# One round of a block's second product ahead of the last four units of the next block's first product; smaller norm groups at the end; ScalarE makes and stores four of six outputs

## The chip, the cores and the metric

The kernel runs on one core of a Trainium2 chip. The metric is device time in microseconds (us), the median of several executions; one further execution was profiled, and all rows below come from that one. Engines are called by the names of the profile: PE (TensorE, matrix products; PEld its weight loads), DVE (VectorE), ACT (ScalarE), POOL (GpSimd) and SP (SyncE, which here only issues DMAs).

## The reference, cut to what matters

`x` is 5120 x 64, `adj` is 5120 x 5120 (105 MB in f32, nearly all zeros).

```
u = par_u[0] * par_u[1] * (diag_u[:, None] * x[:2048] @ W_u) + x[:2048]
i = par_i[0] * par_i[1] * (diag_i[:, None] * x[2048:] @ W_i) + x[2048:]
e = concatenate([u, i])
h = adj @ (adj.T @ e)
h = layernorm(h) * gamma + beta + x
y = layernorm(x + h)
out = layernorm(y + L1(y, adj))
```

`L1` is a graph layer whose edges survive only if softmax scores pass a threshold. The kernel finds the greatest row sum of squares of adj; below a limit no edge can survive, `L1` is zero, and the output is a further layernorm of `y`. With these inputs that is the case, so the program's branch for the message work is never entered.

## The kernel before, in words

Both products need the whole of adj, and adj is read from memory once. It is cut into ten **blocks** of 512 columns (c = 0 to 9). A block is 20 **units** of 512 KB, each two row tiles (256 rows) by 512 columns. On chip there are 40 slots for units, so two blocks fit: even blocks use slots 20 to 39, odd blocks slots 0 to 19, and a unit of block c+2 can be loaded only when its slot's unit of block c is done with.

What happens to a unit, in order:

1. SP issues its load (L977) after the wait `round_done`, that is, after the round that last read the slot.
2. ACT squares it and sums each row (`scan`, L1086), for the limit.
3. PE multiplies it into the **first product** adj.T @ e (`multiply_unit`, L1363), which accumulates over the 20 units of the block in one PSUM bank, `block_bank`.
4. DVE transposes it in place in 32 x 32 pieces (`turn_unit`, L1182), after PE and ACT have read it.

When all 20 units of block c+1 are multiplied, DVE turns the block's sum (`turn_half`, L1191), and ACT and POOL spread it into `col_sum` (`keep_cols`, L1095 and L1022). Then the **second product** of a block, adj @ (adj.T @ e), goes in **rounds** over the transposed units (`multiply_round`, L1382): rounds of 10, 14 and 16 row tiles (5, 7 and 8 units) for blocks 0 to 7, four rounds of 10 for block 8, five rounds of 8 for block 9. Here r0, r1, r2 are the rounds of a block; each leaves its result in four PSUM banks, lower (0 to 3) or upper (4 to 7), and DVE adds it to `h_sum` (`add_round`, L1204). A round waits until the last round in the same banks is added.

Every engine works in the order in which the code is written for it; there is no scheduler. On PE the order is: 20 units of block c+1, then all rounds of block c, then 20 units of block c+2, and so on. Blocks 0 and 1 are interleaved more finely (5 units, r0, 7 units, r1, 8 units, r2 of block 0). After r1 of block 0 PE makes a small product with gamma (L1427), for which ACT waits after its scan of unit 10 of block 1 (L1109).

The end: the rounds of block 9 alternate with `close_tiles` (L1395), which turns eight tiles of `h_sum` into natural rows, minus the mean. Norm group k (8 tiles) then goes: ACT squares (L1113), DVE sums and scales (L1264, L1266), POOL takes the power -1/2 (L1047, `root_c`), DVE multiplies and adds x (L1272, L1276), ACT squares (L1118), DVE sums and scales (L1282, L1285), POOL takes the power (L1052, `root_y`), DVE multiplies (`make_out`, L1293), SP stores (L988). x itself is loaded again once r0 of block 8 has freed its slots (L984), summed by DVE (L1251) and centred by POOL (`center_x`). After the last store has landed SP loads the flag that tells whether the message branch is entered (L407).

Of the kernel before, what the change touches and what calls it, by code (L numbers as in the profile page):

```python
# [7 lines left out]
def adjacency_layers_kernel(nc, x, adj, w_ui, scales, gamma, beta,  # L8
# [13 lines left out]
    P = 128  # L22
# [33 lines left out]
    LGROUPS = T // GT  # L56

# [25 lines left out]
    with ctx:  # L83
# [16 lines left out]
        def setup(width, parts=P):  # L100
# [13 lines left out]
        x_sum, c_sum, var, rstd, y_sum, y_var, y_eps, x1_rstd, scale = (  # L114
            pooled[:, x_at + T * D + T * i:x_at + T * D + T * i + T] for i in range(9))
        ln_at = x_at + T * D + 9 * T

        def ln_buffer(i):
            a = ln_at + GT * D * i
            return pooled[:, a:a + GT * D].rearrange("p (t d) -> p t d", d=D)  # L120

        assert ln_at <= x_at + CH * PARTS[NB - 2][0][1] and ln_at + 8 * GT * D <= x_at + CH * sum(PARTS[NB - 2][1])
        c_sq = [ln_buffer(0), ln_buffer(1)]
        y_sq = [ln_buffer(2), ln_buffer(3)]
        ln_t = [ln_buffer(4), ln_buffer(5)]
        ln_o = [ln_buffer(6), ln_buffer(7)]

# [75 lines left out]
        block_bank = bank[4:6]  # L203
# [36 lines left out]
        c_summed = sem("c_summed")  # L240
# [5 lines left out]
        y_summed = sem("y_summed")  # L246
        y_var_made = sem("y_var_made")
        scale_made = sem("scale_made")
        x1_steps = sem("x1_steps")
        out_made = sem("out_made")  # L250
        out_stored = [sem(f"out_stored{k}") for k in range(2)]
# [111 lines left out]
        def before_in_banks(g):  # L363

            return [r for r in range(g) if upper_banks(r) == upper_banks(g)]

        def nat_of(k):

            return pair[(0, 1, 0, 1, 2)[k]][:, :].rearrange("p (t d) -> p t d", d=2 * D)
# [31 lines left out]
        def over_row(ap):  # L401
            return ap.unsqueeze(2).to_broadcast([P, GT, D])
# [484 lines left out]
        def message_dve(dve):  # L887

            dve.wait_ge(out_stored[0], 16 * ((LGROUPS + 1) // 2))
            dve.wait_ge(out_stored[1], 16 * (LGROUPS // 2))  # L890
# [52 lines left out]
        def message_pool(pool):  # L943

            pool.sem_inc(ln_stored, 16)
            pool.wait_ge(y_summed, LGROUPS)
            for k in range(LGROUPS):
                nc.gpsimd.tensor_scalar(y_eps[:, group_tiles(k)], y_sum[:, group_tiles(k)], 1.0 / D, LN_EPS,
                                        ALU.mult, ALU.add).then_inc(x1_steps, 1)
# [11 lines left out]
        def _(sp):  # L961
# [24 lines left out]
            for k in range(LGROUPS):  # L986
                sp.wait_ge(out_made, k + 1)
                sp.dma_start(tile_rows(out, GT * k, GT), ln_o[k % 2][:, :, :]).then_inc(out_stored[k % 2], 16)  # L988
            sp.wait_ge(out_stored[0], 16 * ((LGROUPS + 1) // 2))
            sp.wait_ge(out_stored[1], 16 * (LGROUPS // 2))  # L990
            with sp.If(edges_may_survive(sp) > 0):
                message_sp(sp)

        @block.gpsimd
        def _(pool):
# [39 lines left out]
            def center_x(k):  # L1035
                xk = x_all[:, group_tiles(k), :]
                pool.wait_ge(x_steps, 1 + 3 * k)
                nc.gpsimd.tensor_tensor(xk, xk, over_row(x_sum[:, group_tiles(k)]), ALU.subtract).then_inc(x_steps, 1)
# [6 lines left out]
            def root_c(k):  # L1045
                pool.wait_ge(var_made, k + 1)
                nc.gpsimd.tensor_tensor(rstd[:, group_tiles(k)], var[:, group_tiles(k)], minus_half[:, :],  # L1047
                                        ALU.pow).then_inc(rstd_made, 1)

            def root_y(k):  # L1050
                pool.wait_ge(y_var_made, k + 1)
                nc.gpsimd.tensor_tensor(scale[:, group_tiles(k)], y_var[:, group_tiles(k)], minus_half[:, :],  # L1052
                                        ALU.pow).then_inc(scale_made, 1)

            for k in range(LGROUPS - 1):
                center_x(k)
            root_c(0)
            pool.wait_ge(rstd_made, 1)
            center_x(LGROUPS - 1)
            pool.wait_ge(x_steps, 1 + 3 * LGROUPS)  # L1060
# [4 lines left out]
            root_c(3)  # L1065
            root_c(4)
            root_y(2)
            root_y(3)
            root_y(4)
            with pool.If(edges_may_survive(pool) > 0):  # L1070
# [3 lines left out]
        def _(act):  # L1074
# [27 lines left out]
            for v in range(1, UNITS):  # L1102
# [4 lines left out]
                if c == 1 and i == UPB[c] // 2:  # L1107
                    act.wait_ge(gamma_turned, 1)
                    act.copy(center[:, D:2 * D], bank[7][:, 0:D]).then_inc(center_kept, 1)  # L1109

            def square_c(k):
                act.wait_ge(nat_made, k + 1)
                nc.scalar.activation(c_sq[k % 2][:, :, :], nat_of(k)[:, :, 0:D],  # L1113
                                     ACT.Square).then_inc(c_squared, 1)

            def square_y(k):
                act.wait_ge(y_made, k + 1)
                nc.scalar.activation(y_sq[k % 2][:, :, :], x_all[:, group_tiles(k), :],  # L1118
                                     ACT.Square).then_inc(y_squared, 1)
# [4 lines left out]
            act.wait_ge(c_summed, 1)  # L1124
# [361 lines left out]
```

## Time and profile before

| | us |
|---|---|
| median of 3 runs | 415.44 (413.74 to 416.66) |
| the profiled execution, device time | 414.27 |
| its span, first to last instruction | 412.5 |
| PE busy | 383.8 (93%) |
| DVE busy | 324.7 (79%) |
| ACT busy | 266.6 (65%) |
| POOL busy | 68.6 (17%) |
| DMA, share of 16 engines by adj and x loads | 72.6% |

The granted PE clock is at full speed (1.00) in each 20 us stretch up to 400 us. No engine is busy all of the time, so the totals alone do not tell what bounds the kernel; the rows below do.

### The profile page before, as it was taken

What the parts mean: (1) busy time and instruction counts of PE and PEld (TensorE: products, weight loads), DVE (VectorE), ACT (ScalarE), POOL (GpSimd) and SP (SyncE); (2) the same over time, 40 slices, a digit from 0 to 9 for tenths busy, and PEclk for the clock granted to TensorE, in tenths of its full rate; (3) what the DMA queues carried; (4) which work ended last, traced back from release to release, by engine and by line L of the source; (5) the groups of instructions that cost most, each with busy time, mean ns of one, the idle gap of its engine ahead of it and who ended that gap; (6) DMA issues with size and microseconds to landing.
All of it is one profiled execution on the core that took longest, in us unless ns stands there. A gap on an engine that the chain in (4) does not pass through costs nothing.

```text
span 412.5 us, 13885 instructions
## 1 busy us (share of the span) xinstructions
PE 383.8 (93%) x6018; PEld 223.2 (54%) x6018; DVE 324.7 (79%) x404; ACT 266.6 (65%) x497; POOL 68.6 (17%) x122
## 2 busy tenths in 40 slices
PE   8987999999999999999999999999999999999940
PEld 7543555565464455546445554644555464668740
DVE  3699769799695979769786966988696697694783
ACT  3696938799888488578848857884785688100220
POOL 2001100303003000300200030011003001169663
PEclk9999999999999999999999999999999999999995
DMA  8999999954992998399389929957992995400002
GB/s 293 386 387 381 386 386 387 382 217 144 388 386 109 322 387 314 114 388 385 138 289 379 354 83 373 387 184 260 385 370 55 392 386 202 130 4 3 29 27 82
DMA packets 56706, 109.87 MB, mean 266 GB/s; under 512 B 3776, under 2 KB 3904, under 8 KB 56640
## 3 DMA queue, kind: packets, MB, share of 16 engines
q1 hardware_dynamic: 56352, 108.84, 72.6%
q8 instruction: 49, 0.80, 0.8%
q10 hardware_dynamic: 288, 0.09, 0.1%
q14 instruction: 17, 0.14, 0.1%
HBM read 107.60 MB, written 1.31 MB: 264 GB/s over the span
## 4 chain that ended last, share of the span: by engine, by line
PE 51%; DMA 23%; SPq 18%; DVE 2%; issue 2%; POOL 1%; ACT 0%; DVEq 0%; ACTq 0%
PE pair L1382 39%; DMA pooled<-in_adj 22%; SPq L977 17%; PE pair L1363 10%; PE pair L1395 2%; DMA pooled<-in_x 2%; POOL pooled L1052 1%; DVE pooled L1204 1%; SPq L968 1%; DVE pooled L1182 1%; SPq L963 1%; POOL pooled L1047 0%; DVE pooled L1272 0%; DVE pooled L1264 0%; DVE pooled L1293 0%
## 5 line engine op out<-in xcount | busy, mean ns | idle before, releaser
L1086 ACT ACTIVATE scratch<-pooled 128x1024 bf16<-128x1024 f32 x200 | 210.5, 1053 | 63.8 <-DMA pooled<-in_adj 61.9
L1182 DVE STREAM_TRANSPOSE pooled<-pooled 128x1024 f32<-128x1024 f32 x200 | 228.8, 1208 | 11.3 <-ACT scratch L1086 8.9
L1363 PE MATMUL pair<-pooled,rows_in 128*64 128x256 f32 x1600 | 186.0, 383 | 10.7 <-DMA pooled<-in_adj 10.3
L1382 PE MATMUL pair<-pooled,col_sum 32*64 32x320 f32 (+3 forms) x4224 | 177.4, 485 | 0.9 <-DVE pooled L1204 0.5
L1363 PEld LDWEIGHTS pair<-pooled,rows_in 128*64 128x64 f32 x1600 | 109.6, 137 | 88.4 <-DMA pooled<-in_adj 31.1
L1382 PEld LDWEIGHTS pair<-pooled,col_sum 32*64 32x64 f32 x4224 | 94.0, 132 | 78.7 <-issue 57.0
L1204 DVE TENSOR_TENSOR pooled<-pooled,pair 128x320 f32<-128x320 f32 (+3 forms) x120 | 58.1, 545 | 44.6 <-PE pair L1382 44.6
L1022 POOL COPY col_sum<-col_half 32x256 f32<-32x256 f32 x80 | 31.6, 394 | 317.6 <-DVE col_half L1191 314.6
L1095 ACT COPY col_sum<-col_half 32x256 f32<-32x256 f32 x80 | 32.2, 403 | 11.1 <-DVE col_half L1191 10.3
L1086 ACT ACTIVATION_READ_ACCUMULATOR scratch<-pooled 128x1 f32 x200 | 37.4, 187 | 0.0
L1113 ACT ACTIVATE pooled<-pair 128x512 f32<-128x512 f32 x5 | 3.0, 598 | 39.3 <-PE pair L1395 39.3
L1191 DVE STREAM_TRANSPOSE col_half<-pair 128x256 f32<-128x256 f32 x10 | 4.4, 438 | 14.4 <-PE pair L1363 14.4
L1395 PEld LDWEIGHTS pair<-center,pooled 128*128 128x128 f32 x80 | 9.2, 192 | 1.5 <-issue 1.5
L1395 PE MATMUL pair<-center,pooled 128*128 128x128 f32 x80 | 10.0, 280 | 0.0
L1047 POOL TENSOR_TENSOR pooled<-pooled,minus_half 128x8 f32<-128x8 f32 x5 | 8.6, 1723 | 6.1 <-DVE pooled L1266 5.9
L1052 POOL TENSOR_TENSOR pooled<-pooled,minus_half 128x8 f32<-128x8 f32 x5 | 8.5, 1710 | 0.7 <-DVE pooled L1285 0.7
L1080 ACT COPY pooled<-pair 128x512 f32<-128x512 f32 x5 | 2.8, 587 | 8.7 <-PE pair L1335 8.7
L1042 POOL TENSOR_TENSOR pooled<-pooled,beta_sb 128x512 f32<-128x512 f32 x5 | 6.7, 1342 | 0.4
L1202 DVE COPY pooled<-pair 128x320 f32<-128x320 f32 (+2 forms) x12 | 6.3, 585 | 0.1
L1118 ACT ACTIVATE pooled<-pooled 128x512 f32<-128x512 f32 x5 | 3.1, 629 | 4.4 <-DVE pooled L1276 4.4
L1156 DVE TENSOR_TENSOR rows_in<-pair,pooled 128x256 f32<-128x256 f32 x10 | 3.7, 410 | 2.9 <-PE pair L1345 2.6
L1345 PE MATMUL pair<-pooled 64*128 64x64 f32 x80 | 5.5, 278 | 0.3 <-ACT pooled L1080 0.3
(47 smaller groups left out, 62.2 us busy)
## 6 DMA issues: line engine op xcount, KB each, us to landing
pooled<-in_adj SPq DMA_DIRECT2D x200, 512.0 KB, 10.1
pooled<-in_x SPq DMA_DIRECT2D x5, 256.0 KB, 3.7
out<-pooled SPq DMA_DIRECT2D x5, 256.0 KB, 2.0
pooled<-in_x SPq DMA_DIRECT2D x1, 768.0 KB, 6.9
pooled<-in_x SPq DMA_DIRECT2D x1, 512.0 KB, 3.7
pooled<-in_w_ui ACTq DMA_DIRECT2D x1, 64.0 KB, 2.9
beta_sb<-in_beta SPq DMA_DIRECT2D x1, 32.0 KB, 9.0
pooled<-in_scales ACTq DMA_DIRECT2D x1, 22.0 KB, 3.2
```

The lines of the kernel that those rows point to most:

```text
L977: sp.dma_start(slots[slot_of(v)].rearrange("p (t k) -> p t k", t=ut), tile_rows(adj, ut * i, ut)[:, :, c0:c0 + WIDTHS[c]]).then_inc(unit_l ...
L1022: kept = nc.gpsimd.tensor_copy(spread_to(c, a, 1, f), spread_from(c, 1, f))
L1042: nc.gpsimd.tensor_tensor(xk, xk, beta_sb[:, :].unsqueeze(1).to_broadcast([P, GT, D]), ALU.add).then_inc(x_steps, 1)
L1047: nc.gpsimd.tensor_tensor(rstd[:, group_tiles(k)], var[:, group_tiles(k)], minus_half[:, :], ALU.pow).then_inc(rstd_made, 1)
L1052: nc.gpsimd.tensor_tensor(scale[:, group_tiles(k)], y_var[:, group_tiles(k)], minus_half[:, :], ALU.pow).then_inc(scale_made, 1)
L1086: nc.scalar.activation(scratch[v % 2][:, :], slots[slot_of(v)], ACT.Square, accum_out=square_sum[:, v:v + 1]).then_inc(unit_scanned, 1)
L1095: kept = act.copy(spread_to(c, a, 0, f), spread_from(c, 0, f))
L1182: nc.vector.transpose(tiles, tiles).then_inc(unit_turned, 1)
L1204: added = nc.vector.tensor_tensor(to, to, share, ALU.add)
L1363: mm = pe.matmul(block_bank[c % 2][half(h), 0:w // 2], rows_in[:, t, :], slots[slot_of(v)][:, at:at + w // 2], start=(t == 0), stop=(t == ...
L1382: mm = pe.matmul(round_banks(g)[a][half(b % 2), 0:w].rearrange("p (t r) -> p t r", r=32), col_sum[c % 2][quadrant(a), b, :], to[quadrant(a ...
L1395: mm = pe.matmul(nat_of(k)[:, i, :], h_sum[:, P * t:P * t + P], center[:, :], start=True, stop=True)
```

## The change

Five things are changed.

1. **Order on PE.** For every block from 1 to 8, r0 of block c stands behind the first 16 units of block c+1 instead of behind all 20; the last four units follow, then r1 and r2. Block 8 now has the rounds 10, 14, 16 too. Block 0's r2 stands behind the first two units of block 2 (`AHEAD`). DVE's order follows.
2. **Banks.** The first product's bank and the banks of the rounds are chosen so that r0 and r1 of a block use the half in which the block's own first product was, r2 the other. So r1 now waits for `add_round` of r0, and r2 for `turn_half` of the block that was just multiplied.
3. **Groups at the end.** Block 9 has rounds and norm groups of 8, 8, 8, 8, 4 and 4 tiles instead of five of 8.
4. **Norm steps.** The factor 1/D is taken into ACT's square, and a 65th column holds epsilon, so that one `tensor_reduce` replaces the reduce and the small `tensor_scalar` (L1266 and L1285 are gone). POOL writes those columns with four small memsets.
5. **Outputs.** The first four output groups are made by ACT, one `activation` of 128 x 64 per tile, and stored from ACT's queue; DVE makes and SP stores only the last two, of 4 tiles. SP loads the flag before it waits for the stores. ACT's wait for gamma moves from behind unit 10 to behind unit 16 of block 1.

The diff, cut to its core:

```diff
-    PARTS = [((0, 10), (10, 14), (24, 16))] * (NB - 2)
-    PARTS += [tuple((t, 10) for t in range(0, T, 10)), tuple((t, 8) for t in range(0, T, 8))]
+    PARTS = [((0, 10), (10, 14), (24, 16))] * (NB - 1)
+    PARTS += [((0, 8), (8, 8), (16, 8), (24, 8), (32, 4), (36, 4))]
+    AHEAD = 2
+        def banks_of_block(c):
+            return c % 2 == 0
         def upper_banks(g):
             c = place_of_round(g)[0]
             if c == NB - 1:
-                return g > LAST
-            return c > 0 and (g - ROUNDS_AT[c]) % 2 == 1
+                return banks_of_block(NB - 2) == (g == LAST)
+            return banks_of_block(c) == (g < ROUNDS_AT[c + 1] - 1)
...
-                if c == 1 and i == UPB[c] // 2:
+                if c == 1 and i == 16:
                     act.wait_ge(gamma_turned, 1)
...
+            def make_out(k):
+                act.wait_ge(scale_made, k + 1)
+                for i in range(norm_size(k)):
+                    t = norm_tiles(k).start + i
+                    made = nc.scalar.activation(ln_o[k % 4][:, i, :], x_all[:, t, :], ACT.Copy, scale=scale[:, t:t + 1])
+                made.then_inc(out_made_act, 1)
+                act.wait_ge(out_made_act, k + 1)
+                store_out(act, k)
...
             def sum_c(k):
                 dve.wait_ge(c_squared, k + 1)
-                tiles = group_tiles(k)
-                nc.vector.tensor_reduce(c_sum[:, tiles], c_sq[k % 2][:, :, :], X, ALU.add).then_inc(c_summed, 1)
-                dve.wait_ge(c_summed, k + 1)
-                nc.vector.tensor_scalar(var[:, tiles], c_sum[:, tiles], 1.0 / D, LN_EPS,
-                                        ALU.mult, ALU.add).then_inc(var_made, 1)
+                nc.vector.tensor_reduce(var[:, norm_tiles(k)], c_sq[k % 2][:, 0:norm_size(k), :], X,
+                                        ALU.add).then_inc(var_made, 1)
...
             for c in range(1, NB - 1):
-                for v in range(UNIT_FIRST[c + 1], UNIT_FIRST[c + 2]):
+                first = UNIT_FIRST[c + 1]
+                for v in range(first + AHEAD if c == 1 else first, first + 16):
                     multiply_unit(v)
-                for g in rounds_of(c):
-                    multiply_round(g)
+                multiply_round(ROUNDS_AT[c])
+                for v in range(first + 16, first + 20):
+                    multiply_unit(v)
+                multiply_round(ROUNDS_AT[c] + 1)
+                multiply_round(ROUNDS_AT[c] + 2)
```

In the middle of the program, PE's order for one block before: L1363 are the units of block c+1 (four matmuls each), L1382 the rounds of block c, 64x320 being r0, 64x448 r1 and 64x512 r2.

```order
L1363 MATMUL pair<-pooled,rows_in 64x256 x80
L1382 MATMUL pair<-pooled,col_sum 64x320 x64
L1382 MATMUL pair<-pooled,col_sum 64x448 x64
L1382 MATMUL pair<-pooled,col_sum 64x512 x64
L1363 MATMUL pair<-pooled,rows_in 64x256 x80
```

The same place now (the lines are L1411 and L1431):

```order
L1411 MATMUL pair<-pooled,rows_in 64x256 x64
L1431 MATMUL pair<-pooled,col_sum 64x320 x64
L1411 MATMUL pair<-pooled,rows_in 64x256 x16
L1431 MATMUL pair<-pooled,col_sum 64x448 x64
L1431 MATMUL pair<-pooled,col_sum 64x512 x64
L1411 MATMUL pair<-pooled,rows_in 64x256 x64
```

r0 moved ahead of 16 matmuls, the last four units. DVE's order for one block before, in the same place (L1182 transposes, L1191 `turn_half`, L1204 `add_round`):

```order
L1182 STREAM_TRANSPOSE pooled<-pooled 128x1024 x13
L1191 STREAM_TRANSPOSE col_half<-pair 128x256
L1182 STREAM_TRANSPOSE pooled<-pooled 128x1024 x2
L1204 TENSOR_TENSOR pooled<-pooled,pair 128x10x32 x4
L1182 STREAM_TRANSPOSE pooled<-pooled 128x1024 x5
L1204 TENSOR_TENSOR pooled<-pooled,pair 128x14x32 x4
L1204 TENSOR_TENSOR pooled<-pooled,pair 128x16x32 x4
```

and now (L1233, L1242, L1255):

```order
L1233 STREAM_TRANSPOSE pooled<-pooled 128x1024 x13
L1255 TENSOR_TENSOR pooled<-pooled,pair 128x10x32 x4
L1233 STREAM_TRANSPOSE pooled<-pooled 128x1024
L1242 STREAM_TRANSPOSE col_half<-pair 128x256
L1233 STREAM_TRANSPOSE pooled<-pooled 128x1024 x5
L1255 TENSOR_TENSOR pooled<-pooled,pair 128x14x32 x4
L1233 STREAM_TRANSPOSE pooled<-pooled 128x1024
L1255 TENSOR_TENSOR pooled<-pooled,pair 128x16x32 x4
```

The add of r0 moved ahead of `turn_half`. The end of PE's program before, from the last round (64x256) on; L1395 is `close_tiles`, L1447 the turn of the greatest sums:

```order
L1382 MATMUL pair<-pooled,col_sum 64x256 x64
L1395 MATMUL pair<-center,pooled 128x128 x16
L1447 MATMUL pair<-ident,part_max 1x128
```

and now, from the first round of 4 tiles (64x128) on; the last 16 closing matmuls are split around a round:

```order
L1431 MATMUL pair<-pooled,col_sum 64x128 x64
L1444 MATMUL pair<-center,pooled 128x128 x8
L1431 MATMUL pair<-pooled,col_sum 64x128 x64
L1444 MATMUL pair<-center,pooled 128x128 x8
L1506 MATMUL pair<-ident,part_max 1x128
```

## Rows read from the trace of the kernel before

**Rows 1.** The page, chain that ended last: shares of the span by line

```profile
PE pair L1382 39%; DMA pooled<-in_adj 22%; SPq L977 17%; PE pair L1363 10%; PE pair L1395 2%; DMA pooled<-in_x 2%; POOL pooled L1052 1%; DVE pooled L1204 1%; SPq L968 1%; DVE pooled L1182 1%; SPq L963 1%; POOL pooled L1047 0%; DVE pooled L1272 0%; DVE pooled L1264 0%; DVE pooled L1293 0%
```

**Rows 2.** The chain in order of time, 200 to 245 us: start, length, what

```profile
202.68 17.46 PE pair L1382 x384
...
226.65 11.43 DMA pooled<-in_adj
...
238.12 1.08 PE pair L1363 x8
```

**Rows 3.** The chain in order of time, 40 to 112 us

```profile
43.56 4.49 PE pair L1382 x128
48.05 6.20 PE pair L1363 x56
54.25 6.20 PE pair L1382 x128
60.81 7.06 PE pair L1363 x64
67.87 7.05 PE pair L1382 x128
74.92 17.42 PE pair L1363 x160
92.34 17.46 PE pair L1382 x384
```

**Rows 4.** The chain over the whole span: the rounds of blocks 2 and 7

```profile
129.66 17.46 PE pair L1382 x384
...
312.14 17.46 PE pair L1382 x384
```

**Rows 5.** ACT in order of time: scans of units 0 and 17, one block

```profile
211.65 1.06 ACT L1086 ACTIVATE scratch<-pooled 128x1024 bf16<-128x1024 f32 x1 [5.13 <-DMA pooled<-in_adj]
...
235.53 1.06 ACT L1086 ACTIVATE scratch<-pooled 128x1024 bf16<-128x1024 f32 x1 [0.20 <-DMA pooled<-in_adj]
```

**Rows 6.** DVE in order of time, the same block

```profile
207.28 1.68 DVE L1204 TENSOR_TENSOR pooled<-pooled,pair 128x320 f32<-128x320 f32 x4 [1.85 <-PE pair L1382]
...
222.56 14.75 DVE L1182 STREAM_TRANSPOSE pooled<-pooled 128x1024 f32<-128x1024 f32 x13
```

**Rows 7.** ACT, then DVE, in order of time around ACT's wait for gamma

```profile
60.84 0.21 ACT L1109 COPY center<-pair 128x64 f32<-128x64 f32 x1 [6.89 <-PE pair L1427]
...
62.21 1.25 DVE L1182 STREAM_TRANSPOSE pooled<-pooled 128x1024 f32<-128x1024 f32 x1 [3.69 <-ACT scratch L1086]
63.38 2.18 DVE L1202 COPY pooled<-pair 128x448 f32<-128x448 f32 x4
65.48 9.11 DVE L1182 STREAM_TRANSPOSE pooled<-pooled 128x1024 f32<-128x1024 f32 x8
```

**Rows 8.** PE in order of time, end: a round of 8 tiles, last closes; PEld of that round

```profile
370.20 3.95 PE L1382 MATMUL pair<-pooled,col_sum 32*64 32x256 f32 x128 [0.52 <-DVE pooled L1204]
...
392.73 3.84 PE L1395 MATMUL pair<-center,pooled 128*128 128x128 f32 x32
...
370.17 3.53 PEld L1382 LDWEIGHTS pair<-pooled,col_sum 32*64 32x64 f32 x128 [0.94 <-issue]
```

**Rows 9.** Groups by line and shape: busy us, mean ns

```profile
L1047 POOL TENSOR_TENSOR pooled<-pooled,minus_half 128x8 f32<-128x8 f32 x5 | 8.6, 1723 | 6.1 <-DVE pooled L1266 5.9
...
L1032 POOL TENSOR_SCALAR pooled<-pooled 128x40 f32<-128x40 f32 x1 | 0.3, 316 | 10.8 <-DVE pooled L1251 10.8
```

**Rows 10.** The end: last output on DVE, landing of the five stores, SP's flag load

```profile
406.26 0.69 DVE L1293 TENSOR_TENSOR pooled<-pooled 128x512 f32<-128x512 f32 x1 [0.55 <-POOL pooled L1052]
...
DMA to landing us min/median/max: 2.0/2.0/3.9
...
L407 SPq TENSOR_LOAD <-flag x1: 472/472/472, 410.9 to 410.9; - x1
L407 SPq FUSED_REGOPS  x1: 191/191/191, 411.4 to 411.4; - x1
```

More of the change, by code:

```diff
@@ L113, in adjacency_layers_kernel, with ln_buffer @@
         x_all = pooled[:, x_at:x_at + T * D].rearrange("p (t d) -> p t d", d=D)
[L114 to L126, printed above, removed]
+        x_sum, var, rstd, y_var, y_eps, x1_rstd, scale = (
+            pooled[:, x_at + T * D + T * i:x_at + T * D + T * i + T] for i in range(7))
+        ln_at = x_at + T * D + 7 * T
+        ln_end = [ln_at]
+        def ln_buffer(width):
+            ln_end[0] += GT * width
+            return pooled[:, ln_end[0] - GT * width:ln_end[0]].rearrange("p (t d) -> p t d", d=width)
+        c_sq = [ln_buffer(D + 1) for _ in range(2)]
+        y_sq = [ln_buffer(D + 1) for _ in range(2)]
+        ln_t = [ln_buffer(D) for _ in range(2)]
+        ln_o = [ln_buffer(D) for _ in range(4)]
+        assert ln_at <= x_at + CH * PARTS[NB - 2][0][1] and ln_end[0] <= x_at + CH * sum(PARTS[NB - 2][1])
         rows_in = sb("rows_in", [P, T, D])
@@ L984, in _ @@
                 sp.dma_start(x_all[:, a:b, :], tile_rows(x, a, b - a)).then_inc(x_again, 16)
[L986 to L991, printed above, removed]
+            for k in range(BY_ACT, NORMS):
+                sp.wait_ge(out_made, k - BY_ACT + 1)
+                store_out(sp, k)
+            survives = edges_may_survive(sp)
+            for k in range(4):
+                sp.wait_ge(out_stored[k], 16 * len(range(k, NORMS, 4)))
+            with sp.If(survives > 0):
                 message_sp(sp)
@@ L1220, in _ @@
                 turn_unit(v)
[L1223 to L1230 removed]
+            for v in range(UNIT_FIRST[1], UNIT_FIRST[1] + 5):
+                turn_unit(v)
+            add_round(0)
+            make_gamma_and_beta()
+            for v in range(UNIT_FIRST[1] + 5, UNIT_FIRST[1] + 12):
+                turn_unit(v)
@@ L1233, in _ @@
+            add_round(1)
+            for v in range(UNIT_FIRST[1] + 12, UNIT_FIRST[1] + 18):
+                turn_unit(v)
+            turn_half(1)
+            for v in range(UNIT_FIRST[1] + 18, UNIT_FIRST[2] + AHEAD):
+                turn_unit(v)
+            add_round(2)
             for c in range(1, NB - 1):
                 first = UNIT_FIRST[c + 1]
-                for v in range(first, first + 13):
-                    turn_unit(v)
-                turn_half(c + 1)
-                for v in range(first + 13, first + 15):
+                for v in range(first + AHEAD if c == 1 else first, first + 13):
@@ L1239, in _ @@
                     turn_unit(v)
                 add_round(ROUNDS_AT[c])
-                if c < NB - 2:
-                    for v in range(first + 15, UNIT_FIRST[c + 2]):
+                turn_unit(first + 13)
+                turn_half(c + 1)
+                if c == NB - 2:
+                    for v in range(first + 14, first + 16):
+                        turn_unit(v)
+                    dve.wait_ge(x_again, 16 * 2)
+                    nc.vector.tensor_reduce(x_sum[:, :], x_all[:, :, :], X, ALU.add).then_inc(x_summed, 1)
+                    add_round(ROUNDS_AT[c] + 1)
+                    for v in range(first + 16, UNITS):
+                        turn_unit(v)
+                else:
+                    for v in range(first + 14, first + 19):
```

212 lines of the change are left out of this document (111 added, 101 removed).

## The prediction

> **What bounds the kernel now.** I first read the chain that ended last. PE holds about half of it, all in products and rounds, and nearly 40% is loads of adj and SP's queue at L977 [rows 1]. So neither PE nor the DMA engines bound it alone; they take turns. The chain in order of time shows how. The rounds of one block are followed by a load, and then by only one unit (eight matmuls) before the next rounds start [rows 2]: the last unit of the product waits for its load, and that load was released by r0 of the block before. The cycle in numbers: r0 starts at 202.68 and lasts 4.49 [rows 3], so it ends at 207.17; the last of the 20 units that it releases lands at 238.08; its unit takes 1.08 and the next r0 starts at 239.20. That is 4.49 + 30.9 + 1.1 = 36.5 us for a block. The rounds of blocks 2 and 7 stand five blocks apart, 129.66 and 312.14 [rows 4]: 182.48/5 = 36.5 again. The same work without waits is 17.42 for 20 units and 17.46 for three rounds [rows 3], 34.9. So a block loses 1.6 us, because the DMA queue stands empty from the last landing to the first landing after r0 (211.65, 4.5 us after r0's end [rows 5]).
>
> **The middle.** r0 now comes four units earlier, 4 x 0.87 = 3.5 us, and frees five slots. The other 15 are freed by r1 and r2, which stand where they stood. What matters more is that the units before the next r0 are 16, not 20. I go round the new cycle from the end of r1. The first landing comes 4.5 us later, as above. The scans of units 0 and 17, which follow the landings, stand 23.88 us apart [rows 5], 1.40 a unit. Units 0 to 4 were released by r0, so units 5 to 15 are needed: unit 15 lands at 4.5 + 10 x 1.40 = 18.5. Then it is multiplied (1.1), r0 follows (4.5), four units (3.5) and r1 (6.2): 33.8 us from r1 to r1. The last four land by 24.1 and are used by 28. The PE's own work is 34.9, so PE becomes the bound with 1.1 us to spare, and the wait is gone.
>
> PE pays something for it: one more change per block between products and rounds. Block 0 shows its price. r0, 7 units, r1, 8 units, r2 take 4.49 + 6.20 + 6.20 + 7.06 + 7.05 = 31.0; 15 units in a row at 0.871 and three rounds in a row are 13.07 + 17.46 = 30.53 [rows 3]. So two more changes cost 0.47, one 0.24, and a block will take 34.88 + 0.24 = 35.1. The Trainium skill has a rule here that speaks against the change: "TensorEngine Tiling (Array Packing)", Key Properties, says that a change of tiling mode drains TensorE, and products and rounds use different modes. The trace agrees in sign, and 0.24 us is what it shows; by that page the eight more changes are a loss of some 2 us, which is in the sum already.
>
> DVE must not take PE's place. In a block it has 20 transposes, of which 13 take 14.75, so 22.7; the adds of r0 and r1 take 1.7 and 2.2, r2's by the same step 2.5, and `turn_half`, a quarter of a transpose's width, some 0.4: 29.5 of 35.1 [rows 6, 7]. The add of r0 is now waited for by r1. DVE starts the 13 transposes 2.5 us into the product, ends them at 17.3, and r0 ends at 18.4: it is there in time, adds until 20.1, and r1 starts at 21.9. r2 waits for `turn_half`, done at some 22.4, and starts at 28. Both waits cost nothing; the cover is 1.8 and 5 us. ACT spreads the columns later than before, while the five early units land. Its scans keep up with landings of 1.40 [rows 5], so 20 take at most 28 of 35.1 and leave 7 for the copies; only transposes queue behind them.
>
> From 109.80 (end of block 1's rounds) to 329.60 (end of block 7's) are six blocks. The first took 147.12 - 109.80 = 37.32, the others 182.48. Six at 35.12 are 210.7 where 219.8 were: **-9.1 us**.
>
> **The start.** r2 of block 0 now needs `turn_half` of block 1. PE reaches it at 60.81 + 10 x 0.88 = 69.6. DVE: ACT stood 6.89 us for gamma and DVE 3.69 for ACT; with the wait behind unit 16 that is gone. So the add of r1 runs from 60.5 to 62.7, six transposes (9.11/8 each) to 69.5, the half to 69.9 [rows 7]. PE waits 0.4 (if ACT still held DVE, up to 3). With the extra change of block 1: **+0.7 us**.
>
> **The end.** Before, from 329.60 to 412.5, 82.9 us; PE is done at 396.57, 67.0 into it [rows 8]. Now: 35.1 to the end of block 8's r2; two rounds of 8 tiles 7.9; three closes and two more such rounds, 2.0 + 3.95 + 2.0 + 3.95 + 2.0 = 13.9, to 56.9; then a round of 4, a close of 8, a round of 4 and two closes of 4. What a round of 4 costs is not in the trace. Half the columns would be 2.0; the same number of instructions at their pace is 3.95. Weight loads are the same 128 in both; in a round of 8 they run for 3.53 us [rows 8]. I take 3.7, nearest to that row. Then 56.9 + 3.7 + 2.0 + 3.7 + 2.1 = 68.4: PE ends 1.4 us later than before. The load of x lies beside r1 and the four units, and no longer stops PE (the 0.52 before the round of 8 goes).
>
> Weighed against a page: the Trainium skill, "TensorE: Matmul & The Clock Gate", LDWEIGHTS, says that a weight load depends on its columns alone, and its Back-to-back issue gap that small matmuls never start closer than 25 ns. By that 128 of them take 3.2 us, 0.5 less than I take each time, and the sum would be 1 us lower.
>
> Behind PE only half as many tiles wait. DVE's operation of 512 columns takes 0.69 [rows 10]; for 256, on ACT too, I take 0.4. So a square and a sum, 0.8, then POOL without a pause: powers for c4, c5, y3, y4, y5. A power of 8 columns takes 1.7. For 4 columns the bounds are 0.85 (half) and 1.7 (no less); a plain POOL operation of 40 columns takes 0.3, so the rest hangs on the columns, and I take 1.0 [rows 9]. So 4 x 1.0 + 1.7 = 5.7, the last output on DVE 0.4, hops 0.5: 75.8. Landing took 2.0 to 3.9 [rows 10]; I take 2.4 for 128 KB. The last store was issued at 407.0 and landed at 410.9; of the 1.6 from there to 412.5 SP's flag load and register work (0.47 + 0.19) now lie beside the landing, leaving 0.9. Sum 79.1, **-3.8 us**. ACT's outputs: its copy of 128 x 64 took 0.21 [rows 7], so 1.7 a group of 8, beside DVE and POOL: nothing. The last such group starts when POOL has made y3, two powers of 4 before the end, so it may take 2.4 before its store comes after SP's. The dropped `tensor_scalar`s, memsets and ACT's store issues lie beside other work and are in the figures above.
>
> **Sum.** -9.1 + 0.7 - 3.8 = -12.2 on the profiled execution's 414.27: 402.1. The median of the runs stands 1.2 above that execution; I add half, **402.7 us**. A measurement here tells about 1% from no change.
>
> **Rivals.**
> - *Rounds of 4 cost by width*: 2.0 instead of 3.7, twice: 399.3. For it speaks that matmuls of 320 columns and more cost by width; against it that 8 tiles (3.95) cost more than 8/10 of r0's 4.49. Chance 0.15.
> - *Powers do not shrink*: four of POOL's five at 1.7, +2.8, 405.5. POOL is the last link either way. Chance 0.14.
> - *A new wait takes back 1 us a block*: PE waits for `add_round` of r0 or for unit 15, since the spare time is only 1.8 and 1.1 us. Seven blocks, 409.7. Chance 0.07.
> - *The change does not do what it says*: PE's queue is strictly in order, so if the moved r0 itself waits (for its columns or its add), units still end last and a block stays at 36.5. Left are start and end, -3.1, 411.8. Against it: its columns are spread over 25 us before. Chance 0.03.
> - *Slower than before*: the loads now come in two bursts, one after r0 and one after r1, and the queue restarts twice. If that made the pace of landing worse, unit 15 would be late: a block takes 19.8 + 10 x pace. At 1.53 it equals PE, at 1.67 the old 36.5, from there the kernel loses. At 1.85 a block takes 38.3, +1.8 in seven blocks, 12.6 - 3.1: 424.4. Against it: scans follow landings at 1.40 across r0, r1 and r2 alike. Chance 0.02.
> - The forecast: 0.59, its own range 400.5 to 405.
>
> **Range and chances.** 398.5 to 408.5 takes in the first two rivals and half of the third. Faster by over 1% (below 411.3) are the forecast and the first three, 0.95; within 1% the fourth, 0.03; slower 0.02.
>
> **What would show it.** In the profile after, PE's idle time behind adj loads in the middle is near zero and r0 starts of neighbouring blocks stand 35.1 apart (34.9 if changes are free, 36.5 if the loads still rule). r2 of block 0 shows a wait of half a microsecond. Rounds of 4 tiles stand with 128 matmuls in some 3.7 us, POOL's powers of 4 columns with 1.0. From PE's last matmul to the end are 11 us, where 15.9 were. The prediction fails if PE is seen waiting for `add_round` or `turn_half` in each block, or if ACT holds a square back behind its outputs.

## The result and the profile after

The changed kernel took **400.49 us** (median, 398.13 to 401.76) beside 415.85 us (413.74 to 416.66) for the kernel before on the same chip. The ratio is **0.963**, 95% interval 0.957 to 0.969. The profiled execution took 400.99 us with a span of 399.2, where 414.27 and 412.5 stood before: 13.3 us less. Of the runs below, two executions, 409.04 (r0 behind 18 units) and 416.96 (more to load, changed order), count as slow, and the ratios leave them out; without them the medians of these two runs are 406.43 and 414.31.

The page of the kernel after, the chain that ended last, shares by engine and by line; it answers to [rows 1]:

```profile
PE 86%; SPq 8%; DMA 3%; issue 1%; ACT 1%; POOL 0%; DVE 0%; ACTq 0%; POOLq 0%
PE pair L1431 44%; PE pair L1411 39%; SPq L1008 6%; DMA pooled<-in_adj 3%; PE pair L1444 3%; SPq L999 1%; SPq L994 1%; ACT pooled L1167 0%; POOL pooled L1084 0%; ACT pooled L1160 0%; SPq L1000 0%; DVE pooled L1332 0%; DVE pooled L1340 0%; PE pair L1477 0%; ACTq L429 0%
```

The loads have fallen from 39% of the chain to 9%, and what is left of them lies ahead of 44 us. The first products (L1411) went from 10% to 39% of it: not more work, but work that used to lie hidden ahead of a late load.

The chain of the kernel after in order of time (start, length, what), which answers to [rows 2 to 4]:

```profile
44.65 4.49 PE pair L1431 x128
...
61.90 8.78 PE pair L1411 x80
70.68 0.39 issue
71.07 7.13 PE pair L1431 x128
78.20 12.24 PE pair L1411 x112
90.44 4.49 PE pair L1431 x128
94.93 3.60 PE pair L1411 x32
98.53 13.07 PE pair L1431 x256
111.60 13.96 PE pair L1411 x128
125.56 4.49 PE pair L1431 x128
...
322.36 13.96 PE pair L1411 x128
336.32 4.49 PE pair L1431 x128
340.81 3.60 PE pair L1411 x32
344.42 19.97 PE pair L1431 x512
```

Between 71 and 388 us the chain stays on PE, but for 1.8 us of "issue" in the last rounds. A block is 16 units, r0, four units, r1 and r2: 13.96 + 4.49 + 3.60 + 13.07 = 35.12 us, without a gap. From r0 of block 2 (125.56) to r0 of block 8 (336.32) are 210.76 us, six times 35.13; the same rounds stood 36.5 apart before [rows 4]. The only wait in the middle is the 0.39 us at 70.68, r2 of block 0 behind `turn_half`.

PE in order of time, kernel after, the end (start, us, what, idle before it); it answers to [rows 8]:

```profile
366.30 3.71 PE L1431 MATMUL pair<-pooled,col_sum 32*64 32x256 f32 x128
...
371.94 4.09 PE L1431 MATMUL pair<-pooled,col_sum 32*64 32x256 f32 x128
...
377.95 1.63 PE L1431 MATMUL pair<-pooled,col_sum 32*64 32x128 f32 x95
381.25 0.70 PE L1431 MATMUL pair<-pooled,col_sum 32*64 32x128 f32 x33 [1.67 <-issue]
381.88 2.05 PE L1444 MATMUL pair<-center,pooled 128*128 128x128 f32 x16
383.87 2.43 PE L1431 MATMUL pair<-pooled,col_sum 32*64 32x128 f32 x128
386.22 2.20 PE L1444 MATMUL pair<-center,pooled 128*128 128x128 f32 x16
```

The first round of 4 tiles needed 1.63 + 0.70 of work, with a stall of 1.67 us in its middle whose releaser is "issue": nothing that the profile shows held PE. Then ACT and POOL behind PE, in order of time, which answer to [rows 9, 10]:

```profile
389.26 2.01 ACT L1167 ACTIVATE pooled<-pooled 128x64 f32<-128x64 f32 x8
391.30 0.34 ACTq L429 DMA_DIRECT2D out<-pooled  x1
391.74 0.72 ACT L1160 ACTIVATE pooled<-pooled 128x256 f32<-128x256 f32 x2 [0.47 <-ACT pooled L1167]
```

```profile
388.95 1.98 POOL L1079 TENSOR_TENSOR pooled<-pooled,minus_half 128x4 f32<-128x4 f32 x2 [0.34 <-DVE pooled L1317]
390.90 3.77 POOL L1084 TENSOR_TENSOR pooled<-pooled,minus_half 128x8 f32<-128x8 f32 x3
```

POOL's last five powers follow each other from 388.95 to 394.67. The second row joins one of 8 columns and two of 4. The chain runs through ACT's outputs (L1167), because the square at 391.74 stood behind them, but POOL was busy until 392.5 and took the result at 392.69, so this costs at most 0.2 us.

### The profile page after: what moved, and what is told of

Same layout as the page of the kernel before. It is cut to its first block, busy times and chain, and to the rows that moved or that the text cites. A ratio compares the mean times of both kernels' runs of the same rounds, so it can differ in the third digit from the quotient of the medians.

```text
span 399.2 us, 13910 instructions
## 1 busy us (share of the span) xinstructions
PE 380.1 (95%) x6018; PEld 222.6 (56%) x6018; DVE 321.5 (81%) x395; ACT 271.9 (68%) x531; POOL 68.5 (17%) x128
## 4 chain that ended last, share of the span: by engine, by line
PE 86%; SPq 8%; DMA 3%; issue 1%; ACT 1%; POOL 0%; DVE 0%; ACTq 0%; POOLq 0%
PE pair L1431 44%; PE pair L1411 39%; SPq L1008 6%; DMA pooled<-in_adj 3%; PE pair L1444 3%; SPq L999 1%; SPq L994 1%; ACT pooled L1167 0%; POOL pooled L1084 0%; ACT pooled L1160 0%; SPq L1000 0%; DVE pooled L1332 0%; DVE pooled L1340 0%; PE pair L1477 0%; ACTq L429 0%
## 5 line engine op out<-in xcount | busy, mean ns | idle before, releaser
L1122 ACT ACTIVATE scratch<-pooled 128x1024 bf16<-128x1024 f32 x200 | 210.1, 1051 | 38.1 <-DMA pooled<-in_adj 36.7
L1233 DVE STREAM_TRANSPOSE pooled<-pooled 128x1024 f32<-128x1024 f32 x200 | 229.6, 1207 | 7.9 <-ACT scratch L1122 7.9
L1411 PE MATMUL pair<-pooled,rows_in 128*64 128x256 f32 x1600 | 181.3, 381 | 4.9 <-DMA pooled<-in_adj 4.8
L1431 PE MATMUL pair<-pooled,col_sum 32*64 32x320 f32 (+4 forms) x4224 | 178.9, 486 | 2.2 <-issue 1.7
L1411 PEld LDWEIGHTS pair<-pooled,rows_in 128*64 128x64 f32 x1600 | 111.7, 137 | 76.1 <-issue 11.7
L1431 PEld LDWEIGHTS pair<-pooled,col_sum 32*64 32x64 f32 x4224 | 90.9, 132 | 83.3 <-issue 66.4
L1255 DVE TENSOR_TENSOR pooled<-pooled,pair 128x320 f32<-128x320 f32 (+4 forms) x120 | 58.4, 548 | 46.7 <-PE pair L1431 46.5
L1152 ACT ACTIVATE pooled<-pair 128x512 f32<-128x512 f32 (+1 forms) x6 | 3.2, 526 | 31.3 <-PE pair L1444 31.3
L1079 POOL TENSOR_TENSOR pooled<-pooled,minus_half 128x8 f32<-128x8 f32 (+1 forms) x6 | 8.6, 1435 | 8.7 <-DVE pooled L1317 8.6
L1242 DVE STREAM_TRANSPOSE col_half<-pair 128x256 f32<-128x256 f32 x10 | 4.4, 441 | 5.7 <-PE pair L1411 5.7
L1084 POOL TENSOR_TENSOR pooled<-pooled,minus_half 128x8 f32<-128x8 f32 (+1 forms) x6 | 8.5, 1430 | 0.1
L1167 ACT ACTIVATE pooled<-pooled 128x64 f32<-128x64 f32 x32 | 8.0, 335 | 0.1
```

Source lines behind the costliest of these rows:

```text
L1079: nc.gpsimd.tensor_tensor(rstd[:, norm_tiles(k)], var[:, norm_tiles(k)], minus_half[:, 0:norm_size(k)], ALU.pow).then_inc(rstd_made, 1)
L1084: nc.gpsimd.tensor_tensor(scale[:, norm_tiles(k)], y_var[:, norm_tiles(k)], minus_half[:, 0:norm_size(k)], ALU.pow).then_inc(scale_made, 1)
L1122: nc.scalar.activation(scratch[v % 2][:, :], slots[slot_of(v)], ACT.Square, accum_out=square_sum[:, v:v + 1]).then_inc(unit_scanned, 1)
L1167: made = nc.scalar.activation(ln_o[k % 4][:, i, :], x_all[:, t, :], ACT.Copy, scale=scale[:, t:t + 1])
L1233: nc.vector.transpose(tiles, tiles).then_inc(unit_turned, 1)
L1255: added = nc.vector.tensor_tensor(to, to, share, ALU.add)
```

## The experiments

They ran in three series; each kernel is compared with the kernel before on its own chip (413.84, 414.52 and 414.27 us). The changed kernel ran again in the second and the third, not in the first, so the first series gives ratios only. Each trace is one execution.

**The changed kernel again.** 

> The changed kernel itself, for comparison on the chip of this series: its ratio to before should be 0.957 to 0.969 as in the first result, with blocks 35.1 us apart. If it comes out near 0.975 instead, the chip matters and the runs with the early gamma wait and with r0 behind 18 units lost less than they seemed to (they gave 0.976 and 0.980).

> The changed kernel again, on the chip of this series, as the base of the three runs beside it: 0.957 to 0.974 of before.

401.15 us (398.86 to 401.96), ratio 0.968 (0.962 to 0.974), and 401.16 us (399.59 to 402.70), ratio 0.970 (0.963 to 0.977). So the gain is 3 to 3.7%, and two kernels that differ by less than some 0.7% can't be told apart here. In the first repeat the first round of 4 tiles had a stall of 1.40 (time in which PE does nothing and waits for nothing that the profile shows, "issue"); in the second it had none:

```profile
378.46 2.10 PE L1431 MATMUL pair<-pooled,col_sum 32*64 32x128 f32 x128
380.49 2.05 PE L1444 MATMUL pair<-center,pooled 128*128 128x128 f32 x16
```

From start to start that round took 2.03 us.

**The end alone.** Order and banks of before, with the groups, the norm steps and ACT's outputs of the change. The core of the edit against the changed kernel:

```diff
-    PARTS = [((0, 10), (10, 14), (24, 16))] * (NB - 1)
-    PARTS += [((0, 8), (8, 8), (16, 8), (24, 8), (32, 4), (36, 4))]
+    PARTS = [((0, 10), (10, 14), (24, 16))] * (NB - 2)
+    PARTS += [tuple((t, 10) for t in range(0, T, 10)), ((0, 8), (8, 8), (16, 8), (24, 8), (32, 4), (36, 4))]
...
-                if c == 1 and i == 16:
+                if c == 1 and i == UPB[c] // 2:
```

> The end of the changed kernel (groups of 8, 8, 8, 8, 4, 4, fused norm steps, ScalarE's outputs, flag loaded early) behind the middle of the kernel before (old order, old banks, block 8 in four rounds, gamma wait at unit 10). My theory: the two parts are additive, and the end alone brings what the two traces show from the end of block 7's rounds on, 82.9 - 76.8 = 6 us, less what block 8 brought of it (its unit waits 1.8, a shorter tail of rounds 0.5), so 3 to 4.5 us: about 411.5 against 415.5 of before, with blocks still 36.5 us apart. Rival: the end gained only because the middle delivers x and the rounds earlier (before, PE waited 0.5 us behind the sum of x), then this run is within 1 us of before.

411.63 us (409.66 to 414.38, 10 runs), ratio 0.994 (0.991 to 0.998): 0.6%, some 2.4 us, less than the 3 to 4.5 that were expected. Its chain in order of time shows the middle of before, a load and eight matmuls ahead of each set of rounds, here 36.35 us apart and 36.6 in the mean of blocks 2 to 7:

```profile
130.28 17.46 PE pair L1430 x384
...
154.16 11.35 DMA pooled<-in_adj
...
166.63 17.46 PE pair L1430 x384
```

Its end, from 330.7 to 411.5, is 80.8 us long, 2.1 less than before. Both of its rounds of 4 tiles stalled, here in the order of time of PE:

```profile
388.93 1.57 PE L1430 MATMUL pair<-pooled,col_sum 32*64 32x128 f32 x89
392.19 0.91 PE L1430 MATMUL pair<-pooled,col_sum 32*64 32x128 f32 x39 [1.69 <-issue]
...
396.96 1.14 PE L1430 MATMUL pair<-pooled,col_sum 32*64 32x128 f32 x56 [0.59 <-issue]
```

**The order alone.** Order, banks, gamma wait and the fused norm steps of the change; five groups of 8, DVE's outputs and the late load of the flag of before. The core of the edit:

```diff
-    PARTS += [((0, 8), (8, 8), (16, 8), (24, 8), (32, 4), (36, 4))]
+    PARTS += [tuple((t, 8) for t in range(0, T, 8))]
...
-    BY_ACT = 4
+    BY_ACT = 0
```

> The middle of the changed kernel (order, banks, three rounds for block 8, gamma wait at unit 16) with the end of before: five groups of 8, VectorE makes and SP stores all outputs, flag loaded behind the stores; the fused norm steps stay. My theory: the middle brings 8.3 us to the end of block 7 (35.1 instead of 36.5 a block) and about 2 us in block 8, so 405 to 406, and together with the run of the end alone it makes the whole 15 us. Rival (the parts overlap: the end would hide part of what the middle gains, or the reverse): the two gains together miss the whole by more than 2 us.

404.94 us (403.25 to 405.20), ratio 0.975 (0.968 to 0.982). This part carries four fifths of the gain of the two runs. They add up within the noise: 0.6% and 2.5% are 3.1%, where the whole gave 3.0 to 3.7%. But the fused norm steps are in both runs, so what they bring is counted twice, and no run has them alone. Its blocks stand 35.13 us apart, except one of 36.17 with a late load. Block 7's rounds end at 322.74 and the span at 403.4, so its end is 80.7 us long, where 82.9 stood before and 76.8 after. So in these traces 2.2 of the end's 6.1 us come with the order and the fused norm steps (PE's 0.52 us behind the load of x [rows 8] is one part), and the small groups and ACT's outputs bring 3.9 on top of them. With the order of before all the steps of the end together brought 2.1 us (above), so their worth hangs on the order.

**The wait for gamma left at unit 10.**

```diff
-                if c == 1 and i == 16:
+                if c == 1 and i == 10:
```

> The changed kernel with one number back: ScalarE waits for gamma behind unit 10 of block 1, not 16. My theory: ScalarE stands about 7 us, VectorE's 7th transpose of that stretch waits until 63, the add of r1 and turn_half come 3 us later, and PE's wait for turn_half before r2 of block 0 grows from 0.4 to about 3 us; the whole kernel is about 2.7 us longer (403.3 against 400.5), since PE is the bound from there on and nothing gives it back. Rival: the later loads have room enough behind r2 of block 0, so the delay is taken up by block 1 and the time stays within 1 us.

> The early gamma wait again, now beside the changed kernel on the same chip. In its first trace PE waited 3.17 us for turn_half, 2.8 more than the changed kernel. If that is all, it is 2.8 us (0.7%) longer than the changed kernel here; the first series gave 4 to 6 us against a changed kernel of another chip. If it is 5 us again, something behind r2 of block 0 loses as well (the later loads of block 2, or late loads in block 3).

406.10 us (402.15 to 407.86), ratio 0.976 (0.968 to 0.985), and again 404.25 us (403.03 to 405.91), ratio 0.975 (0.969 to 0.982), 3.1 us more than the changed kernel beside it. The repeat's PE, in order of time:

```profile
73.49 8.82 PE L1431 MATMUL pair<-pooled,col_sum 32*64 32x512 f32 x128 [3.17 <-DVE pooled L1233]
```

r2 of block 0 waits 3.17 us where it waited 0.39, and then takes 8.82 us instead of 7.13. That is not more work: behind the wait PE's granted clock fell to half, 1.2 instead of 2.4 GHz, from 74.2 to 77.6 us. The windows view of that stretch (times; busy us and number of instructions of PE, PEld, DVE, ACT and POOL; granted clock; DMA share; GB/s):

```profile
74.20:77.60 3.40, 3.40 (x40) 1.54 (x32) 1.44 (x2) 3.30 (x8) 2.45 (x7) 0.50 0.85 311
```

3.4 us at half the clock cost 1.7, which is 8.82 - 7.13. The first run's trace shows the same: a wait of 3.17, half the clock from 73.2 to 76.6, and 8.43 us for r2. In the changed kernel, which waits 0.39 there, the clock stayed at 1.00. From r2 on the blocks follow each other at 35.13. So this execution, the slowest of its four, lost 2.8 us by the longer wait and 1.7 by the clock behind it, 4.5 in all; the medians stand 3.1 apart. The 0.4 us of the forecast rests on the moved line.

**r0 behind 18 units instead of 16.**

```diff
-                for v in range(first + AHEAD if c == 1 else first, first + 16):
+                for v in range(first + AHEAD if c == 1 else first, first + 18):
                     multiply_unit(v)
                 multiply_round(ROUNDS_AT[c])
-                for v in range(first + 16, first + 20):
+                for v in range(first + 18, first + 20):
```

DVE adds r0 behind 14 transposes instead of 13, directly ahead of `turn_half`.

> The changed kernel with r0 of a block behind 18 units of the next product instead of 16 (VectorE adds it behind 14 transposes instead of 13). My theory (a cycle of loads: from the end of r1 4.5 us to the first landing, 1.36 to 1.40 a unit, then unit, r0, the remaining units, r1): unit 17 lands 20.8 to 21.3 after r1, then 1.1 + 4.5 + 1.7 + 6.2 = 34.3 to 34.8, just below PE's 35.1, so the block stays at 35.1 to 35.4 us, with loads as PE's last wait now and then and a small wait of r1 for the add of r0 (0 to 0.2): 400.5 to 402.5. Rival: any unit behind r0 is enough to hide the loads, and the time is 400.5 as before with no wait at all; other rival: the bank handover costs a full add (1.7 us less 1.7 of the two units, plus hops) in each block, 0.3 x 8 = 2.4 us or more.

> r0 behind 18 units again, now beside the changed kernel. The cycle of loads has some 0.3 us to spare by the average pace, and the traces show single landings 1.2 us late; so by my theory it loses in the executions in which they fall badly, 1 to 6 us more than the changed kernel, with a wider spread (402 to 409 in the first series, the profiled one being its fastest). Rival (18 is as good as 16, and the first series saw its chip): within 1 us.

406.61 us (402.34 to 409.04, 6 runs), ratio 0.980 (0.973 to 0.987), and 406.97 us (405.43 to 407.35), ratio 0.982 (0.975 to 0.988), 5.8 us more than the changed kernel beside it; 400.5 to 402.5 was expected. Of the seven distances between its r0 in the repeat four are 35.3 to 36.0 us and three 36.5 to 37.5; the mean is 36.1. In the long ones PE waits again for single units ahead of r0:

```profile
162.00 1.08 PE L1410 MATMUL pair<-pooled,rows_in 128*64 128x256 f32 x8 [0.26 <-DMA pooled<-in_adj]
163.34 1.08 PE L1410 MATMUL pair<-pooled,rows_in 128*64 128x256 f32 x8 [0.26 <-DMA pooled<-in_adj]
164.35 4.56 PE L1430 MATMUL pair<-pooled,col_sum 32*64 32x320 f32 x128
```

So having some units behind r0 is not enough; their number counts. Each unit more ahead of r0 adds one landing to the cycle and takes 0.88 us of product out of its rest. With 16, unit 15 came 0.4 us before PE wanted it (below), so that cycle was 34.7 us. At the 1.56 us for a landing that were measured there, 18 units make it 34.7 + 2 x (1.56 - 0.88) = 36.1. That the mean is 36.1 too is partly chance. The seven distances hold 6.8 us more than seven of 35.13. The loads account for half of it, some 3.4. Rounds that took 13.91 and 14.80 us (with a stall of 0.69) instead of 13.14 account for 2.4, and a longer way from r0 to r1 and through r1 and r2, 0.13 in each block, for the rest. Why the rounds stretched is not shown; the granted clock was 1.00 there.

**r0 behind 12 units.** The same edit with 12, DVE adding r0 behind 10 transposes.

> The changed kernel with r0 behind 12 units of the next product instead of 16, eight behind it (VectorE adds it behind 10 transposes). My theory: PE is the bound at 35.1 us a block, so a profiled execution without late loads is as long as the changed kernel's, within 1 us. But the cycle of loads has 1.1 us to spare behind 16 units and about 3 us behind 12 (unit 11 lands at 4.5 + 6 x 1.4 = 12.9, then 1.1 + 4.5 + 7.0 + 6.2 = 31.7), and the traces show single loads that land 1.2 us or more late; so the waits for adj in the middle vanish in every execution, and the spread of the times shrinks. The rival theory is that all that matters is that units stand behind r0: then 12, 16 and 18 give the same.

399.95 us (399.50 to 400.66), ratio 0.966 (0.961 to 0.971), beside 401.15 for 16 units. The intervals overlap, so it is not shown to be faster. PE has no wait for adj behind 84 us in its trace, as was expected. Its times spread over 1.2 us, the 16's over 3.1 in the same series. Its r0 stand 35.12 or 35.13 us apart, the first two here:

```profile
86.22 4.49 PE pair L1432 x128
...
121.34 4.49 PE pair L1432 x128
```

The cycle by loads is 4 x (1.56 - 0.88) = 2.7 us shorter than with 16 units. That brings no time, since PE's work is the floor.

**More to load.** From block 2 on, each unit's load is followed in SP's queue by a copy of 64 KB that nothing needs, an eighth more bytes; once with the changed order, once with that of before.

```diff
+                if c >= 2:
+                    sp.dma_start(tile_rows(pruned, ut * i, 1)[:, 0, c0:c0 + P],
+                                 tile_rows(adj, ut * i, 1)[:, 0, c0:c0 + P]).then_inc(spare_loaded, 16)
```

> The changed kernel with 64 KB more DMA traffic behind each unit's load from block 2 on, a copy of a part of adj into a scratch tensor in memory that nothing reads (it also writes 64 KB, so the cost is between 12% and 25% of a unit's load: a landing every 1.53 to 1.70 us). My theory, from the cycle 19.8 + 10 x pace: 35.1 to 36.8 us a block, so 0 to 12 us longer in seven blocks. Rival (PE alone bounds it, the loads are hidden whatever they cost): no change.

> The kernel before with the same extra traffic. My theory: its cycle holds 20 landings in a row, 4.5 + 4.5 + 19 x pace + 1.1, so each block grows by 19 times the pace's growth: 39.2 to 42.4 us instead of 36.5, 19 to 41 us longer in all, at least twice what the changed kernel loses. Rival (both are bound by the DMA engines' total, and the change only removed a constant idle time): both grow alike.

Changed order: 414.70 us (410.28 to 416.96, 8 runs), ratio 0.999 (0.995 to 1.003), 13.5 us more than without the copies, a little beyond the expected 0 to 12. Order of before: 442.09 us, ratio 1.068 (1.061 to 1.075), 27.6 us more. Chains in order of time, the changed order first, then that of before:

```profile
126.73 4.49 PE pair L1435 x128
...
346.94 4.49 PE pair L1435 x128
```

```profile
214.30 17.46 PE pair L1386 x384
...
254.54 17.46 PE pair L1386 x384
...
294.81 17.46 PE pair L1386 x384
```

A block takes 36.7 us in the first (220.2/6) and 40.3 in the second: 1.6 and 3.8 more than without. The order of before pays for every slower landing; the changed one has a little cover first, and beyond it pays for the ten steps from unit 5 to unit 15, where the other pays for nineteen. The sizes fit: 3.8/19 is 0.20 us for a landing, and 10 x 0.20 less the 0.4 of cover (below) is 1.6.

**Block 9's rounds of 8 in two passes of 4.** Four rounds are made of 256 narrow matmuls instead of 128:

```diff
+                cuts = 2 if c == NB - 1 and nt == 8 else 1
+                for cut in range(cuts):
+                    t0, t1 = nt // cuts * cut, nt // cuts * (cut + 1)
```

> The changed kernel with each of block 9's four rounds of 8 tiles made in two passes of 4 tiles (128 matmuls and weight loads each, same results), which measures what a round of 4 costs. If the cost goes by width, as the one undisturbed round of 4 seen so far suggests (2.03 us, against 3.64 for 8 tiles), two passes take 4.1 us and the kernel grows by 4 x 0.4 = 1.8 us at most. If it goes by the number of instructions (3.6 a pass), it grows by 14 us. If the stall inside a round of 4 (1.4 to 1.7 us without any releaser in four of five traces) is PE running out of instructions that come too slowly, eight passes in a row must show more and longer such stalls, some 1.5 us in every second pass, 6 us in all.

409.85 us (two runs), 8.7 us more than the changed kernel beside it, ratio 0.990 (0.982 to 0.998). PE in order of time:

```profile
363.06 2.08 PE L1434 MATMUL pair<-pooled,col_sum 32*64 32x128 f32 x128 [1.50 <-issue]
366.52 1.86 PE L1434 MATMUL pair<-pooled,col_sum 32*64 32x128 f32 x111 [1.38 <-issue]
368.31 2.05 PE L1447 MATMUL pair<-center,pooled 128*128 128x128 f32 x16
```

A pass of 128 takes 2.1 us each time, so two are 4.1 to 4.2 beside 3.64 for a round of 8: four rounds, 2 us. The rest is stalls. The groups by line and shape, this kernel and then the kernel after (busy us, mean ns, idle before, releaser):

```profile
L1434 PE MATMUL pair<-pooled,col_sum 32*64 32x128 f32 x1280 | 21.6, 274 | 7.9 <-issue 7.9
```

```profile
L1431 PE MATMUL pair<-pooled,col_sum 32*64 32x128 f32 x256 | 4.8, 277 | 1.7 <-issue 1.7
```

7.9 us instead of 1.7, and one more stall of 1.07 in a close: 7.3 more in stalls. Together 9.3, about the 8.7 measured. The trace of the changed kernel of the same series has one stall, 0.39: against it there are 8.6 more in stalls, 10.6 in all, and these two executions are 10.3 us apart. The clock was 1.00 throughout.

## Why the prediction was right, and where its sizes were off

The time lay in the range, 2.2 us faster than the 402.7 named, and the mechanism was the one forecast. That it came so close is partly luck. On the profiled execution 402.1 was predicted and 400.99 measured: the middle and the start gave -8.3 where -8.4 was predicted, the end -6.1 instead of -3.8, and a later r0 of block 0, which has nothing in the sum, took 1.1 of the difference back. The other 1.1 is the step to the median: 0.6 was added, and the median stood 0.5 below the profiled execution. By its own steps:

- **The block.** 35.1 us predicted, 35.13 measured, with the wait for the load gone. From r0 of block 0 to the end of block 7's rounds it took 329.60 - 43.56 = 286.0 before and 322.36 - 44.65 = 277.7 after: -8.3 us, where -9.1 + 0.7 = -8.4 was predicted. r0 of block 0 itself stood 1.1 us later than before; in the kernels of the experiments it stood between 43.1 and 44.7 (44.0 was seen with either order), so an effect of the change on it is not shown.
- **The price of one more change between products and rounds**, 0.24 us, was right: 34.88 + 0.24 is the block.
- **The start.** PE's wait for `turn_half` was predicted as 0.4 and is 0.39; with the gamma wait at unit 10 it is 3.17, the "up to 3" of the prediction. That the clock falls behind such a wait and costs up to 1.7 more, the prediction did not have.
- **The new waits in each block** don't exist (the rival at 0.07, as far as `add_round` goes). DVE is the one that waits now; in order of time, kernel after:

```profile
130.16 1.68 DVE L1255 TENSOR_TENSOR pooled<-pooled,pair 128x320 f32<-128x320 f32 x4 [1.30 <-PE pair L1431]
...
133.71 0.45 DVE L1242 STREAM_TRANSPOSE col_half<-pair 128x256 f32<-128x256 f32 x1 [0.71 <-PE pair L1411]
```

  The add of r0 ended at 131.8 and r1 started at 133.66: the cover of 1.8 us is there, exactly.
- **The spare time of the loads** was overestimated. ACT's scans of units 5, 6 and 15 of block 3 in order of time, kernel after:

```profile
108.75 1.06 ACT L1122 ACTIVATE scratch<-pooled 128x1024 bf16<-128x1024 f32 x1 [1.05 <-DMA pooled<-in_adj]
...
111.22 1.06 ACT L1122 ACTIVATE scratch<-pooled 128x1024 bf16<-128x1024 f32 x1 [1.32 <-DMA pooled<-in_adj]
...
124.33 1.06 ACT L1122 ACTIVATE scratch<-pooled 128x1024 bf16<-128x1024 f32 x1 [0.20 <-DMA pooled<-in_adj]
```

  The ten steps take 15.58 us, 1.56 a unit instead of 1.40: two of them, such as the first shown, are 2.5 us long. Unit 15 was there at 124.33 and PE wanted it at 125.56 - 0.87 = 124.7, so the spare time was 0.4 us, not 1.1 (1.3 against the prediction's own 35.1). The first of the landings came 4.0 us behind r1, not 4.5, or it would have been gone. The rival "a new wait takes back 1 us a block" came close: in four of six other traces with r0 behind 16 units one block with a wait for a load was 0.6 to 1.1 us longer. With 18 units it came true in three of seven blocks.
- **The end** is the step that failed in size: -3.8 us predicted, to 79.1; measured 399.2 - 322.36 = 76.8, **-6.1**. The mis-sized term is "a round of 4 tiles, 3.7 us, nearest to the row of 8". Undisturbed it is 2.03, a little over half of a round of 8: the matmuls cost nearly by width, as the rival at 0.15 said, and the ground against it, that "8 tiles cost more than 8/10 of r0", came from a round of 8 in 3.95 us [rows 8], where the shortest ones now run at 3.64 (8/10 of r0 are 3.59). The rival's 399.3 was nearer to the measured time than the forecast. What it lacked was something that no part of the prediction had: the stalls "issue". The two rounds took 3.93 and 2.35, together 6.3 where 7.4 was predicted and 4.1 would be undisturbed. The rounds of 8 give the other 1.3: two 6.9 instead of 7.9, and two with three closes 13.6 instead of 13.9. So PE ends 66.1 into the end, not 68.4.
- **Behind PE**, 10.7 us predicted and 399.2 - 388.43 = 10.8 measured, but two misses cancel in it: the last output was made 6.7 us behind PE's last matmul, not 7.4, and from there to the end were 4.1, not 3.3 (the last two stores landed in 3.0 us in the median, where 2.4 was taken). Powers of 4 columns take 1.0 as taken. ACT makes a group of 8 in 2.0 us, not 1.7, which costs nothing. It did hold a square back, the sign named for a failure: DVE had its input ready at 391.05, and ACT, busy with outputs and their store, began it at 391.74. Behind POOL's queue at most 0.2 us of that is left.

The Trainium skill, "TensorE: Matmul & The Clock Gate", Back-to-back issue gap, was weighed with 3.2 us for 128 matmuls. That section gives its floor of about 25 ns for matmuls of 1 to 64 columns. These have 128 columns and took 2.03 us, 15.9 ns each in the mean, so the floor does not hold for matmuls of 32 rows and 64 output partitions that are spread over four row quadrants and two column halves of the array, as these are.

**What stays open.** That PE runs out of instructions in the stalls is argued, not shown. For it: they have no releaser, they multiply with the number of narrow matmuls (two passes), and they sit where matmuls are densest: a round of 4 runs 128 in 2.03 us, 63 per us, the product's 80 in 8.78, 9 per us. Their place is not random: in eight of the ten traces of kernels with the changed order and a first round of 4 tiles that round stalls behind its 95th of 128 matmuls, by 1.40 us in five and by 1.67 in three (after matmul 89 with the order of before); the other two have no stall in it. That speaks for something that hangs on the place in the program, but does not tell what. Against it: three of 0.2, 0.4 and 0.7 us also stood in the middle, in rounds of 320 columns and more. The DMA view shows the instruction queue moving 0.11 MB between 365 and 395 us both in the two-pass kernel and after, so it tells nothing. Why two landings a block come 1.2 us late was not found either.

## What to carry to other kernels

When a cycle of "round frees slot, load, unit, round" is longer than the engine's own work, count how many loads stand between the release and the round that makes the next release, and reorder so that fewer do; once the cycle is shorter than the engine's work, a further move earns no time, only a margin against late loads. Look then for what the new order waits for elsewhere: one early wait on another engine, ACT's for gamma, would have taken back some 3 of 13 us, in part through the clock that fell behind PE's wait. Smaller last groups pay behind the last matmul, as long as the matmuls don't become so short that PE starts to stall.

## What the runs showed of the hardware

- 128 f32 matmuls of 32 rows x 128 columns, each with its weight load of 64 columns, go in 2.03 us, 15.9 ns each; with 256 columns in 3.64 us.
- With such short matmuls PE stalls for 0.4 to 1.9 us with nothing to wait for, in seven places in one kernel with 1280 of them.
- After PE had waited 3.17 us, its granted clock was 0.50 for 3.4 us, which cost up to 1.7 us; after stalls of up to 1.92 us (two passes) it stayed at 1.00.
- The landings of 512 KB after an empty queue are not even: mostly 1.3 to 1.4 us apart, but two of the first ones 2.5 (one block read).
- ACT's `activation` of 128 x 64 with a scale per partition follows its predecessor every 0.25 us; POOL's power takes 1.65 us for 8 columns and 1.0 for 4.
